# Four plane buffers for the table lookup, paid for with shared bias, Silu and output buffers

## Chip, cores and metric

One Trainium2 chip, all 8 of its cores. Each core runs the same program on its own part of the data. The metric is the device time of the slowest core, in microseconds (us). Shorter is better.

## What is computed

One transformer layer on x of shape (2, 4096, 2048), f32. After a layer norm, linear attention and a gated feed-forward are both applied to the normalised input and added to x. The feed-forward's weights come as indices (0 to 15) into a table of 16 values.

```python
xn = layernorm(x)                                # over the last axis, 2048
Q = relu(xn @ Wq.T + bq) * decay                 # 16 heads of 128
K = relu(xn @ Wk.T + bk) * decay
V = xn @ Wv.T + bv
KV = einsum('bhnd,bhne->bhde', K, V); Ksum = K.sum(axis=2)
Z = 1 / (einsum('bhnd,bhd->bhn', Q, Ksum) + 1e-6)
attn = (einsum('bhnd,bhde->bhne', Q, KV) * Z) @ Wo.T + bo
gate = xn @ lut[gate_idx].T                      # (5504, 2048) indices
up   = xn @ lut[up_idx].T
ffn  = (silu(gate) * up) @ lut[down_idx].T       # (2048, 5504) indices
out  = x + attn + ffn
```

## The kernel before

Each core owns 1024 rows of x, in 8 tiles of 128. It also computes K and V for all 4096 rows of its batch (32 tiles), so that no core needs anything of another. The work goes through stages with a barrier (`s_ph`) between them:

- Start: K and V weights are loaded and cast, and the biases `bk_bf`, `bv_bf` (L274, L275), each one row on one partition, are copied by ScalarE.
- A (K/V stage): for each of 32 tiles layer norm, transposes, K and V projections (L507, L519) and the sums over rows.
- B1: layer norm and transposes of the core's own 8 tiles, by VectorE and TensorE.
- B2: Q projection, 32 units of 16 matmuls (L699) and a bias matmul (L702), with `bq_bf` (L656); VectorE clears negative values (L717).
- B3: attention output for 8 tiles.
- B5a: output projection, 16 units of 32 matmuls (L911), with `bo_bf` (L853).
- B4 (gate/up stage): 43 chunks `ic` of 128 hidden units. For each and for both halves `h2` of the columns: 16 gate matmuls (L993), 16 up matmuls (L999), Silu by ScalarE (L1014), the multiplication by VectorE (L1026). TensorE's results have two buffers, so it is at most two chunks ahead of VectorE (L990).
- B5b (last stage): 4 quarters `q` of the output columns, for each 8 x 43 matmuls (L1104), then the addition of x (L1118) for 8 tiles `t` and the store (L1131).

**Weights from the table.** Beside all this the index blocks `k` = 0 to 128 (43 each for gate, up and down) are turned into bf16 weights of 128 x 2048, written to memory and read again in B4 and B5b. GpSimd (`g_front`) loads the indices of block k+1 (L126), casts those of block k (L134) and stores the weights of block k-1 (L171). There are two ways to look a block up:

- `g_vec`, VectorE alone (blocks 0 to 29 in stage A, 109 to 128 in B4): for each of 16 values a plane (the table value where the index equals v, else 0) and an addition, 15 pairs of L159 and L162.
- `g_vec_a` with `g_pe`, assisted by TensorE (79 blocks: 10 in B1, 22 in B2, 22 in B3, 25 in B5a): VectorE makes plane v (L205), TensorE adds it into PSUM with 4 matmuls against the identity (L222). `s_pl` counts planes made, `s_pm` planes consumed. After 16 planes VectorE copies PSUM to `wts` (L211). There are two plane buffers, so VectorE waits at L204 for the plane before the last. In all of these stages the loops on VectorE and TensorE carry the same blocks at the same places, between their other work, each engine's queue in program order.

In B4 the Silu results have one buffer for each half; ScalarE waits at L1013 for the multiplication of the same half of the chunk before. In B5b there are eight output buffers `xo8`. SyncE's queue holds for each quarter the 43 loads of weights (L1074), each waiting for the one before and for the matmuls three back, and then the 8 loads of x (L1084), each waiting for the one before it (L1083) and, from the second quarter on, for the store of the same tile of the quarter before (L1081). GpSimd's queue holds the stores, VectorE's the additions.

Of the kernel before, what the change touches and what calls it, by code (L numbers as in the profile page):

```python
# [16 lines left out]
D = 2048  # L17
# [16 lines left out]
def build():  # L34
# [38 lines left out]
    with es0:  # L73
# [14 lines left out]
        wts = [es0.enter_context(nc.sbuf_tensor(f"wt{i}", [128, D], BF16)) for i in range(2)]  # L88
        planes = [es0.enter_context(nc.sbuf_tensor(f"plane{i}", [128, D], BF16)) for i in range(2)]
        wt2 = es0.enter_context(nc.sbuf_tensor("wt2", [128, D], BF16))  # L90
# [106 lines left out]
        def g_vec_a(vector, k):  # L197
            a = AORD[k]
            gb = gbs[k % 2]
            vector.wait_ge(s_gc, VEC_IDX[k] + 1)  # L200
            for v in range(16):
                p = a * 16 + v
                if p >= 2:
                    vector.wait_ge(s_pm, p - 1)  # L204
                i = vector.tensor_scalar(planes[v % 2][:], gb[:], float(v),  # L205
                                         lutb[:, v : v + 1], ALU.is_equal, ALU.mult)
                inc(i, "s_pl", s_pl, 1)
            vector.wait_ge(s_pm, (a + 1) * 16)
            if k > 1:
                vector.wait_ge(s_go, 16 * (k - 1))  # L210
            i = vector.tensor_copy(wts[k % 2][:], PS_ACC[0][:])  # L211
            inc(i, "s_gv", s_gv, 1)

        def g_pe(tensor, k):
            a = AORD[k]
            ps_acc = PS_ACC[0]
            for v in range(16):
                tensor.wait_ge(s_pl, a * 16 + v + 1)
                if v == 0:
                    tensor.wait_ge(s_gv, k)  # L220
                for j4 in range(4):
                    i = tensor.matmul(ps_acc[:, j4 * 512 : (j4 + 1) * 512], eye_sb[:],  # L222
                                      planes[v % 2][:, j4 * 512 : (j4 + 1) * 512],
                                      start=(v == 0), stop=(v == 15), skip_group_check=True)
                inc(i, "s_pm", s_pm, 1)
# [47 lines left out]
        ps_tr = esA.enter_context(nc.psum_tensor("ps_tr", [128, 1024], BF16))  # L273
        bk_bf = esA.enter_context(nc.sbuf_tensor("bk_bf", [1, D], BF16))  # L274
        bv_bf = esA.enter_context(nc.sbuf_tensor("bv_bf", [1, D], BF16))  # L275

# [378 lines left out]
        xtb2 = [xtb2_0, xtb2_0]  # L655
        bq_bf = esB2.enter_context(nc.sbuf_tensor("bq_bf", [1, D], BF16))  # L656
        wbig = arena[:, 32768:65536].rearrange("p (a b) -> p a b", a=DC)
# [194 lines left out]
        xtb5 = [xtb5_0, xtb5_0]  # L852
        bo_bf = esB5a.enter_context(nc.sbuf_tensor("bo_bf", [1, D], BF16))  # L853
        wohalf = arena[:, 16384:32768].rearrange("p (a b) -> p a b", a=DC)
# [103 lines left out]
        w2b = [w2sb_, wt2]  # L958
        silu_sb = [esB4.enter_context(nc.sbuf_tensor(f"silu{i}", [128, 512], F32)) for i in range(2)]
        ps_g = [esB4.enter_context(nc.psum_tensor(f"ps_g{i}", [128, 1024], F32)) for i in range(2)]  # L960
# [4 lines left out]
        with nc.Block() as blk:  # L965
# [41 lines left out]
            def _(scalar):  # L1007
                bwait(scalar)
                for ic in range(IC):
                    for h2 in range(2):  # L1010
                        scalar.wait_ge(s_mm, MB4 + 4 * ic + 2 * h2 + 1)
                        if ic > 0:
                            scalar.wait_ge(s_ve, VB4 + 2 * (ic - 1) + h2 + 1)  # L1013
                        i = scalar.activation(silu_sb[h2][:], ps_g[ic % 2][:, h2 * 512 : (h2 + 1) * 512],  # L1014
                                              AF.Silu)
                        inc(i, "s_sc", s_sc, 1)
# [30 lines left out]
        w3qb = [arena[:, i * 512 : (i + 1) * 512] for i in range(NW3)]  # L1047
        xo8 = [esB5b.enter_context(nc.sbuf_tensor(f"xo8_{i}", [128, 512], F32)) for i in range(8)]
        ps8 = [esB5b.enter_context(nc.psum_tensor(f"ps8_{i}", [128, 512], F32)) for i in range(8)]
# [7 lines left out]
        with nc.Block() as blk:  # L1057
# [6 lines left out]
            def _(sync):  # L1064
                bwait(sync)
                for q in range(4):
# [10 lines left out]
                    for t in range(8):  # L1077
                        m = 8 * q + t
                        if q > 0:
                            n = (8 * (q - 1) + t - t % 2) // 2 + 1  # L1080
                            sync.wait_ge(s_oa[t % 2], 16 * n)  # L1081
                        if m >= 1:
                            sync.wait_ge(s_xo, XO0 + 16 * m)  # L1083
                        d = sync.dma_start(out=xo8[t][:],  # L1084
                                           in_=xo[t * 128 : (t + 1) * 128, q * 512 : (q + 1) * 512])
# [26 lines left out]
            def _(vector):  # L1112
                bwait(vector)
                for q in range(4):
                    vector.wait_ge(s_mm, MB5 + (IC + 1) * (q + 1))
                    for t in range(8):
                        vector.wait_ge(s_xo, XO0 + 16 * (8 * q + t + 1))  # L1117
                        i = vector.tensor_tensor(xo8[t][:], ps8[t][:], xo8[t][:], ALU.add)  # L1118
                        inc(i, "s_ve", s_ve, 1)
# [3 lines left out]
            def _(gpsimd):  # L1123
                bwait(gpsimd)
                for q in range(4):
                    for t in range(8):
                        gpsimd.wait_ge(s_ve, VB5 + 8 * q + t + 1)  # L1127
                        n = (8 * q + t - t % 2) // 2
                        if n > 0:
                            gpsimd.wait_ge(s_oa[t % 2], 16 * n)  # L1130
                        d = gpsimd.dma_start(out=y[t * 128 : (t + 1) * 128, q * 512 : (q + 1) * 512],  # L1131
                                             in_=xo8[t][:])
                        inc(d, f"s_out{t % 2}", s_oa[t % 2], 16)
# [69 lines left out]
```

## Time and profile before

| | us |
|---|---|
| timed runs, median (2 runs, 4982.36 to 4986.58) | 4984.47 |
| profiled execution | 5030.28 |
| its span, slowest core (core 3) | 5028.7 |
| spans of the 8 cores | 4965.5 to 5028.7 |
| start and K/V stage | 0 to about 1516 |
| B1, B2, B3, B5a | 1516 to about 3755 |
| B4 | 3755 to about 4508 |
| B5b | 4508 to 5028.7 |

PE is TensorE, PEld its weight loads, DVE VectorE, ACT ScalarE, POOL GpSimd, SP SyncE; a "q" behind a name is the engine's sequencer. PEclk is the granted TensorE clock, 1.00 being 2.4 GHz and 0.50 being 1.2 GHz. A row of instructions names line and operation, then what is written and read (out<-in, buffer numbers left out), then shapes and count. `[0.42 <-PE ps_acc L222]` behind a row of the timeline means that the engine sat idle for 0.42 us before it and that the instruction named released it. `x2` merges two instructions that follow each other; a merged row's length runs from the first start to the last end. The ends of matmuls are modelled and overlap the next one's start. A row of busy time by stretch gives the stretch (us from the start of the span) and its length, then the busy time (and instructions) of PE, PEld, DVE, ACT and POOL, then PEclk, the busy share of the DMA engines, and GB/s.

### The profile page before, as it was taken

Reading aid. Unit: us, or ns where it says so; the run is one execution under the profiler, and the core shown is the slowest. Engines: PE = TensorE matmul, PEld = TensorE weight load, DVE = VectorE, ACT = ScalarE, POOL = GpSimd, SP = SyncE. Lnnn points to the kernel's source line nnn. Section 1 sums busy time; section 2 is a strip of 40 time slices with the busy share of each in tenths; the row PEclk is TensorE's granted clock in tenths of the full one; section 3 lists DMA queues with packets and bytes.
Section 4 is the critical chain, followed back from the end, with each engine's and each line's share of the span. In section 5 each row is a group of like instructions: output and inputs, shape, how many; then the busy total and the mean of one; then the engine's idle time right before and its main releaser. Section 6 shows DMA issues by size and latency. Waiting matters only on the chain. (4 is left out here: it accounts for less than half of the span.)

```text
span 5028.7 us, 46175 instructions; the slowest of 8 cores (4965.5 to 5028.7 us)
## 1 busy us (share of the span) xinstructions
PE 3768.2 (75%) x16705; PEld 1494.3 (30%) x16705; DVE 3015.7 (60%) x3433; ACT 522.9 (10%) x715; POOL 411.6 (8%) x428
## 2 busy tenths in 40 slices
PE   0699998989885625888877772895889898866666
PEld 0233333333332211333322220332324333322222
DVE  0677786888855623666666662674767898970000
ACT  4222222222210011000000001001000000000000
POOL 0000000000000000111111110111110000000000
PEclk9888889999997767999888886998999999979988
DMA  7211111111101121000000002012112222212222
GB/s 245 82 40 45 44 45 38 45 45 44 51 21 54 51 95 71 32 32 32 32 32 32 32 32 82 33 44 76 37 50 80 84 86 87 83 52 78 78 76 76
DMA packets 91161, 297.99 MB, mean 59 GB/s; under 512 B 11639, under 2 KB 33655, under 8 KB 79673
## 3 DMA queue, kind: packets, MB, share of 16 engines
q1 hardware_dynamic: 59484, 185.19, 11.1%
q0 software_dynamic: 31456, 109.86, 6.3%
q8 instruction: 139, 2.28, 0.2%
q14 instruction: 82, 0.67, 0.0%
HBM read 218.98 MB, written 76.02 MB: 59 GB/s over the span
## 5 line engine op out<-in xcount | busy, mean ns | idle before, releaser
L222 PE MATMUL ps_acc<-plane,eye_sb 128*128 128x512 bf16 x5056 | 1299.1, 402 | 247.7 <-DVE plane L205 181.2
L205 DVE TENSOR_SCALAR plane<-gb,lutb 128x2048 bf16<-128x2048 bf16 x1264 | 1012.7, 807 | 553.2 <-PE ps_acc L222 502.3
L162 DVE TENSOR_TENSOR wt<-wt,plane 128x2048 bf16<-128x2048 bf16 x750 | 918.6, 1225 | 57.9 <-issue 2.6
L222 PEld LDWEIGHTS ps_acc<-plane,eye_sb 128*128 128x128 bf16 x5056 | 440.4, 101 | 1097.4 <-issue 814.0
L507 PE MATMUL ps_rot<-wk_bf,xnT_sb 128*128 128x512 bf16 x2048 | 557.0, 434 | 43.6 <-ACT xnT_sb L471 43.6
L159 DVE TENSOR_SCALAR plane<-gb,lutb 128x2048 bf16<-128x2048 bf16 x750 | 559.6, 746 | 0.0
L519 PE MATMUL ps_rot<-wv_bf,xnT_sb 128*128 128x512 bf16 x2048 | 489.1, 394 | 0.0
L1104 PE MATMUL ps<-arena 128*128 128x512 bf16 x1376 | 326.7, 382 | 79.5 <-DMA arena<-w2h 79.3
L1118 DVE TENSOR_TENSOR xo<-ps,xo 128x512 f32<-128x512 f32 x32 | 22.1, 692 | 496.5 <-PE ps L1104 426.2
L507 PEld LDWEIGHTS ps_rot<-wk_bf,xnT_sb 128*128 128x128 bf16 x2048 | 211.8, 108 | 351.7 <-issue 238.6
L519 PEld LDWEIGHTS ps_rot<-wv_bf,xnT_sb 128*128 128x128 bf16 x2048 | 194.9, 100 | 258.8 <-issue 102.1
L134 POOL CAST gb<-gi 128x2048 bf16<-128x2048 int8 x129 | 245.3, 1902 | 9.7 <-DMA gi<-g 7.2
L211 DVE CAST wt<-ps_acc 128x2048 bf16<-128x2048 f32 x79 | 181.0, 2291 | 106.4 <-PE ps_acc L222 106.4
L911 PE MATMUL ps_w<-arena 128*128 128x512 bf16 x512 | 117.2, 389 | 131.7 <-ACT arena L895 131.7
L699 PE MATMUL ps_q<-arena 128*128 128x512 bf16 x512 | 118.7, 386 | 120.8 <-ACT arena L684 120.8
L1104 PEld LDWEIGHTS ps<-arena 128*128 128x128 bf16 x1376 | 125.0, 98 | 281.8 <-issue 158.6
L993 PE MATMUL ps_g<-arena,KV_sb 128*128 128x512 bf16 x672 | 172.6, 416 | 46.6 <-DVE arena L1026 46.6
L993 PE MATMUL ps_g<-arena,w1sb 128*128 128x512 bf16 x704 | 173.4, 403 | 38.3 <-DVE arena L1026 28.6
L497 PE MATMUL ps_tr<-eye_sb,xn_bf 128*128 128x128 bf16 x512 | 42.8, 232 | 203.8 <-DVE xn_bf L259 134.4
L999 PE MATMUL ps_u<-arena,w2sb 128*128 128x512 bf16 x704 | 159.1, 379 | 0.0
L229 DVE TENSOR_REDUCE st<-xt 128x1 f32<-128x2048 f32 x32 | 73.1, 2286 | 141.7 <-DMA xt<-xb 135.8
L999 PE MATMUL ps_u<-arena,wt 128*128 128x512 bf16 x672 | 151.9, 379 | 0.0
(92 smaller groups left out, 1798.9 us busy)
## 6 DMA issues: line engine op xcount, KB each, us to landing
xt<-xb SPq DMA_DIRECT2D x32, 1024.0 KB, 4.9
gi<-g POOLq DMA_DIRECT2D x86, 256.0 KB, 3.8
w0h<-wt POOLq DMA_DIRECT2D x43, 512.0 KB, 3.0
w1h<-wt POOLq DMA_DIRECT2D x43, 512.0 KB, 3.0
w2h<-wt POOLq DMA_DIRECT2D x43, 512.0 KB, 3.0
arena<-w2h SPq DMA_DIRECT2D x172, 128.0 KB
xt<-wkT SPq DMA_DIRECT2D x16, 1024.0 KB, 5.6
xt<-wvT SPq DMA_DIRECT2D x16, 1024.0 KB, 5.5
```

The source lines that it names most:

```text
L134: i = eng.tensor_copy(gbs[k % 2][:], gi[k % 2][:])
L159: vector.tensor_scalar(planes[v % 2][:], gb[:], float(v), lutb[:, v : v + 1], ALU.is_equal, ALU.mult)
L162: vector.tensor_tensor(wt[:], wt[:], planes[v % 2][:], ALU.add)
L205: i = vector.tensor_scalar(planes[v % 2][:], gb[:], float(v), lutb[:, v : v + 1], ALU.is_equal, ALU.mult)
L211: i = vector.tensor_copy(wts[k % 2][:], PS_ACC[0][:])
L222: i = tensor.matmul(ps_acc[:, j4 * 512 : (j4 + 1) * 512], eye_sb[:], planes[v % 2][:, j4 * 512 : (j4 + 1) * 512], start=(v == 0), stop=(v ...
L507: tensor.matmul(ps_rot[j % 2][:], xnT_sb[:, dc * 128 : (dc + 1) * 128], wk_bf[:, dc, j * 512 : (j + 1) * 512], start=(dc == 0), stop=False)
L519: tensor.matmul(ps_rot[j % 2][:], xnT_sb[:, dc * 128 : (dc + 1) * 128], wv_bf[:, dc, j * 512 : (j + 1) * 512], start=(dc == 0), stop=False)
L699: tensor.matmul(pq[:], wbig[:, dc, qc * 128 : (qc + 1) * 128], xnT_own[:, dc, h2 * 512 : (h2 + 1) * 512], start=(dc == 0), stop=False)
L993: i = tensor.matmul(pg[:, h2 * 512 : (h2 + 1) * 512], w1b[ic % 2][:, dc * 128 : (dc + 1) * 128], xnT_own[:, dc, h2 * 512 : (h2 + 1) * 512] ...
L999: i = tensor.matmul(pu[:, h2 * 512 : (h2 + 1) * 512], w2b[ic % 2][:, dc * 128 : (dc + 1) * 128], xnT_own[:, dc, h2 * 512 : (h2 + 1) * 512] ...
L1104: i = tensor.matmul(ps8[t][:], hT_sl(ic, slice(t * 128, (t + 1) * 128)), w3qb[j % NW3], start=False, stop=(ic == IC - 1), skip_group_check ...
```

## The change

The planes get four buffers instead of two, and VectorE waits for the plane four back. The room comes from elsewhere: `bk_bf` and `bv_bf` become the first partition of planes 2 and 3, `bq_bf` and `bo_bf` that of `wt2`; both Silu halves share one buffer, and ScalarE waits for the multiplication just before; the output buffers of the last stage are four instead of eight, and the load of x for tile t waits for the store four tiles back. The instructions and their number are the same on every engine; only buffers and the values waited for differ.

```diff
--- before.py
+++ after.py
@@ -86,7 +86,7 @@
         gi = [es0.enter_context(nc.sbuf_tensor(f"gi{i}", [128, D], I8)) for i in range(2)]
         gbs = [es0.enter_context(nc.sbuf_tensor(f"gb{i}", [128, D], BF16)) for i in range(2)]
         wts = [es0.enter_context(nc.sbuf_tensor(f"wt{i}", [128, D], BF16)) for i in range(2)]
-        planes = [es0.enter_context(nc.sbuf_tensor(f"plane{i}", [128, D], BF16)) for i in range(2)]
+        planes = [es0.enter_context(nc.sbuf_tensor(f"plane{i}", [128, D], BF16)) for i in range(4)]
         wt2 = es0.enter_context(nc.sbuf_tensor("wt2", [128, D], BF16))
 
         KV_sb = es0.enter_context(nc.sbuf_tensor("KV_sb", [128, H * 128], BF16))
@@ -200,9 +200,9 @@
             vector.wait_ge(s_gc, VEC_IDX[k] + 1)
             for v in range(16):
                 p = a * 16 + v
-                if p >= 2:
-                    vector.wait_ge(s_pm, p - 1)
-                i = vector.tensor_scalar(planes[v % 2][:], gb[:], float(v),
+                if p >= 4:
+                    vector.wait_ge(s_pm, p - 3)
+                i = vector.tensor_scalar(planes[v % 4][:], gb[:], float(v),
                                          lutb[:, v : v + 1], ALU.is_equal, ALU.mult)
                 inc(i, "s_pl", s_pl, 1)
             vector.wait_ge(s_pm, (a + 1) * 16)
@@ -220,7 +220,7 @@
                     tensor.wait_ge(s_gv, k)
                 for j4 in range(4):
                     i = tensor.matmul(ps_acc[:, j4 * 512 : (j4 + 1) * 512], eye_sb[:],
-                                      planes[v % 2][:, j4 * 512 : (j4 + 1) * 512],
+                                      planes[v % 4][:, j4 * 512 : (j4 + 1) * 512],
                                       start=(v == 0), stop=(v == 15), skip_group_check=True)
                 inc(i, "s_pm", s_pm, 1)
 
@@ -271,8 +271,8 @@
         ps_ks = esA.enter_context(nc.psum_tensor("ps_ks", [128, H], F32))
         ps_rot = [esA.enter_context(nc.psum_tensor(f"ps_rot{b}", [128, 512], F32)) for b in range(2)]
         ps_tr = esA.enter_context(nc.psum_tensor("ps_tr", [128, 1024], BF16))
-        bk_bf = esA.enter_context(nc.sbuf_tensor("bk_bf", [1, D], BF16))
-        bv_bf = esA.enter_context(nc.sbuf_tensor("bv_bf", [1, D], BF16))
+        bk_bf = planes[2][0:1, 0:D]
+        bv_bf = planes[3][0:1, 0:D]
 
         with nc.Block() as blk:
             @blk.sync
@@ -653,7 +653,7 @@
         esB2 = contextlib.ExitStack()
         xtb2_0 = esB2.enter_context(nc.sbuf_tensor("xtb2_0", [128, D], F32))
         xtb2 = [xtb2_0, xtb2_0]
-        bq_bf = esB2.enter_context(nc.sbuf_tensor("bq_bf", [1, D], BF16))
+        bq_bf = wt2[0:1, 0:D]
         wbig = arena[:, 32768:65536].rearrange("p (a b) -> p a b", a=DC)
         ps_q = [esB2.enter_context(nc.psum_tensor(f"ps_q{i}", [128, 512], F32)) for i in range(4)]
         ps_acc2 = esB2.enter_context(nc.psum_tensor("ps_acc2", [128, 2048], F32))
@@ -850,7 +850,7 @@
         esB5a = contextlib.ExitStack()
         xtb5_0 = esB5a.enter_context(nc.sbuf_tensor("xtb5_0", [128, 1024], F32))
         xtb5 = [xtb5_0, xtb5_0]
-        bo_bf = esB5a.enter_context(nc.sbuf_tensor("bo_bf", [1, D], BF16))
+        bo_bf = wt2[0:1, 0:D]
         wohalf = arena[:, 16384:32768].rearrange("p (a b) -> p a b", a=DC)
         ps_w = [esB5a.enter_context(nc.psum_tensor(f"ps_w{i}", [128, 1024], F32)) for i in range(2)]
         ps_acc5 = esB5a.enter_context(nc.psum_tensor("ps_acc5", [128, 2048], F32))
@@ -956,7 +956,8 @@
         w2sb_ = esB4.enter_context(nc.sbuf_tensor("w2sb", [128, D], BF16))
         w1b = [w1sb_, KV_sb]
         w2b = [w2sb_, wt2]
-        silu_sb = [esB4.enter_context(nc.sbuf_tensor(f"silu{i}", [128, 512], F32)) for i in range(2)]
+        silu1 = esB4.enter_context(nc.sbuf_tensor("silu0", [128, 512], F32))
+        silu_sb = [silu1, silu1]
         ps_g = [esB4.enter_context(nc.psum_tensor(f"ps_g{i}", [128, 1024], F32)) for i in range(2)]
         ps_u = [esB4.enter_context(nc.psum_tensor(f"ps_u{i}", [128, 1024], F32)) for i in range(2)]
 
@@ -1009,8 +1010,8 @@
                 for ic in range(IC):
                     for h2 in range(2):
                         scalar.wait_ge(s_mm, MB4 + 4 * ic + 2 * h2 + 1)
-                        if ic > 0:
-                            scalar.wait_ge(s_ve, VB4 + 2 * (ic - 1) + h2 + 1)
+                        if ic > 0 or h2 > 0:
+                            scalar.wait_ge(s_ve, VB4 + 2 * ic + h2)
                         i = scalar.activation(silu_sb[h2][:], ps_g[ic % 2][:, h2 * 512 : (h2 + 1) * 512],
                                               AF.Silu)
                         inc(i, "s_sc", s_sc, 1)
@@ -1045,7 +1046,7 @@
         esB5b = contextlib.ExitStack()
         NW3 = 3
         w3qb = [arena[:, i * 512 : (i + 1) * 512] for i in range(NW3)]
-        xo8 = [esB5b.enter_context(nc.sbuf_tensor(f"xo8_{i}", [128, 512], F32)) for i in range(8)]
+        xo8 = [esB5b.enter_context(nc.sbuf_tensor(f"xo8_{i}", [128, 512], F32)) for i in range(4)]
         ps8 = [esB5b.enter_context(nc.psum_tensor(f"ps8_{i}", [128, 512], F32)) for i in range(8)]
 
         VB5, SB5, MB5 = C["s_ve"], C["s_sc"], C["s_mm"]
@@ -1076,12 +1077,12 @@
                         inc(d, "s_x0", s_xp[0], 16)
                     for t in range(8):
                         m = 8 * q + t
-                        if q > 0:
-                            n = (8 * (q - 1) + t - t % 2) // 2 + 1
+                        if m >= 4:
+                            n = (m - 4 - t % 2) // 2 + 1
                             sync.wait_ge(s_oa[t % 2], 16 * n)
                         if m >= 1:
                             sync.wait_ge(s_xo, XO0 + 16 * m)
-                        d = sync.dma_start(out=xo8[t][:],
+                        d = sync.dma_start(out=xo8[t % 4][:],
                                            in_=xo[t * 128 : (t + 1) * 128, q * 512 : (q + 1) * 512])
                         inc(d, "s_xo", s_xo, 16)
                 bdone(sync)
@@ -1115,7 +1116,7 @@
                     vector.wait_ge(s_mm, MB5 + (IC + 1) * (q + 1))
                     for t in range(8):
                         vector.wait_ge(s_xo, XO0 + 16 * (8 * q + t + 1))
-                        i = vector.tensor_tensor(xo8[t][:], ps8[t][:], xo8[t][:], ALU.add)
+                        i = vector.tensor_tensor(xo8[t % 4][:], ps8[t][:], xo8[t % 4][:], ALU.add)
                         inc(i, "s_ve", s_ve, 1)
                 bdone(vector)
 
@@ -1129,7 +1130,7 @@
                         if n > 0:
                             gpsimd.wait_ge(s_oa[t % 2], 16 * n)
                         d = gpsimd.dma_start(out=y[t * 128 : (t + 1) * 128, q * 512 : (q + 1) * 512],
-                                             in_=xo8[t][:])
+                                             in_=xo8[t % 4][:])
                         inc(d, f"s_out{t % 2}", s_oa[t % 2], 16)
                 gpsimd.wait_ge(s_oa[0], 16 * 16)
                 gpsimd.wait_ge(s_oa[1], 16 * 16)
```

## Rows read from the trace of the kernel before

**Rows 1.** The cores view: span and mean granted clock of cores 0 and 3.

```profile
core 0: 4976.6 us, clock 0.879
...
core 3: 5028.7 us, clock 0.882
```

**Rows 2.** Busy time by stretch: 180 to 620 us, core 0, then core 3.

```profile
180.00:620.00 440.00, 393.74 (x2024) 169.67 (x2024) 374.44 (x396) 104.48 (x165) 32.68 (x33) 0.93 0.14 47
...
180.00:620.00 440.00, 399.61 (x1821) 161.88 (x1820) 334.52 (x354) 94.29 (x149) 29.67 (x30) 0.81 0.11 40
```

**Rows 3.** Costliest groups: L222; count | busy us, mean ns | idle us <-releaser.

```profile
L222 PE MATMUL ps_acc<-plane,eye_sb 128*128 128x512 bf16 x5056 | 1299.1, 402 | 247.7 <-DVE plane L205 181.2
```

**Rows 4.** Timeline of full-clock bursts, PE and DVE: start, us, engine, what, idle before.

```profile
1995.94 1.41 DVE L205 TENSOR_SCALAR plane<-gb,lutb 128x2048 bf16<-128x2048 bf16 x2
1996.94 16.12 PE L222 MATMUL ps_acc<-plane,eye_sb 128*128 128x512 bf16 x64 [1.72 <-DVE plane L205]
...
2000.11 1.62 DVE L205 TENSOR_SCALAR plane<-gb,lutb 128x2048 bf16<-128x2048 bf16 x2 [0.42 <-PE ps_acc L222]
...
2002.14 1.61 DVE L205 TENSOR_SCALAR plane<-gb,lutb 128x2048 bf16<-128x2048 bf16 x2 [0.42 <-PE ps_acc L222]
...
3715.19 16.14 PE L222 MATMUL ps_acc<-plane,eye_sb 128*128 128x512 bf16 x64
```

**Rows 5.** Timeline of PE alone: K/V stage, a half-clock start, then projections of B2.

```profile
187.51 4.37 PE L507 MATMUL ps_rot<-wk_bf,xnT_sb 128*128 128x512 bf16 x16
...
2019.93 17.50 PE L222 MATMUL ps_acc<-plane,eye_sb 128*128 128x512 bf16 x64 [3.09 <-DVE plane L205]
2037.27 3.62 PE L699 MATMUL ps_q<-arena 128*128 128x512 bf16 x16
2040.81 0.38 PE L702 MATMUL ps_q<-ones_bf,bq_bf 1*128 1x512 bf16 x1
```

**Rows 6.** Stretch of the gate/up stage B4, core 3, same columns.

```profile
3755.00:4508.00 753.00, 632.06 (x2752) 276.33 (x2752) 643.11 (x707) 52.63 (x87) 59.29 (x60) 0.92 0.24 82
```

**Rows 7.** Waits of the whole run: who waited for whom, us, times, longest.

```profile
ACT silu L1014 <- DVE arena L1026: 390.7, 19, 22.3
...
PE ps_g L993 <- DVE arena L1026: 75.2, 18, 5.8
...
DVE arena L1026 <- PE ps_u L999: 72.8, 10, 14.8
```

**Rows 8.** Source view of L222: durations ns min/median/max; what its idle time waited for.

```profile
L222 PE MATMUL ps_acc<-plane,eye_sb x5056: 376/378/634, 1521.2 to 3751.9; 128*128 128x512 bf16 x195
...
  DVE plane L205: 181.2, 86
```

**Rows 9.** Timeline around a cast of GpSimd in a burst of B5a.

```profile
3262.89 1.90 POOL L134 CAST gb<-gi 128x2048 bf16<-128x2048 int8 x1
3262.97 3.04 DVE L205 TENSOR_SCALAR plane<-gb,lutb 128x2048 bf16<-128x2048 bf16 x2 [0.72 <-PE ps_acc L222]
...
3265.50 1.67 PE L222 MATMUL ps_acc<-plane,eye_sb 128*128 128x512 bf16 x7 [1.77 <-DVE plane L205]
```

**Rows 10.** Timeline of B4 behind a table block: DVE and ACT.

```profile
3836.29 1.28 DVE L1026 TENSOR_TENSOR arena<-silu,ps_u 128x512 bf16<-128x512 f32 x2 [0.26 <-issue]
...
3837.07 1.19 ACT L1014 ACTIVATE silu<-ps_g 128x512 f32<-128x512 f32 x2 [20.85 <-DVE arena L1026]
...
3837.84 1.28 DVE L1026 TENSOR_TENSOR arena<-silu,ps_u 128x512 bf16<-128x512 f32 x2 [0.27 <-ACT silu L1014]
...
3839.05 1.16 DVE L157 TENSOR_SCALAR wt<-gb,lutb 128x2048 bf16<-128x2048 bf16 x1
```

**Rows 11.** Timeline of B5b, first quarter: a store's issue, the fourth addition.

```profile
4616.09 0.54 POOL L1131 DMA_DIRECT2D y<-xo  x1 [110.80 <-DVE xo L1118]
...
4622.14 0.69 DVE L1118 TENSOR_TENSOR xo<-ps,xo 128x512 f32<-128x512 f32 x1 [2.07 <-DMA xo<-xo]
```

**Rows 12.** Source view of L1131: time from the issue of a store to landing.

```profile
DMA to landing us min/median/max: 2.3/2.9/4.4
```

## The prediction

> **What bounds the kernel now.** I read the views in this order: spans and clocks of the cores, the costliest groups, then the timeline inside each stage that the change touches.
>
> The cores differ, and this must be cleared away first. The profiled core is 3, some 50 us longer than core 0 [rows 1]. In 180 to 620 us, inside the K/V stage, core 3 was granted 0.81 of the TensorE clock and did 1821 matmuls where core 0 did 2024 [rows 2]. That is 203 fewer, at about 0.22 us each 44 us, nearly the whole difference. The stage is not touched by the change. The timed runs (median 4984.5) agree with the cores that escaped this. So I work out microseconds gained or lost on core 3 and subtract them both from its own time (span 5028.7 plus 1.6 around it, 5030.3) and from the median; the profile lies 45.8 above the median, and that offset has nothing to do with the change.
>
> The assisted table stages (B1, B2, B3, B5a) hold 79 bursts of 16 planes, 64 matmuls each: 5056 matmuls at L222, 1299 us of TensorE [rows 3]. VectorE makes a plane, TensorE adds it into PSUM with four identity matmuls, and the two are alone with each other. A burst at full clock shows who sets the pace [rows 4]: TensorE takes 16.12 us for 64 matmuls without a recorded pause, yet VectorE's pairs of planes start at 2000.11 and 2002.14, 2.03 us apart, so 1.017 us for each plane. TensorE alone could do better. Sixteen dense matmuls take 3.62 us and a lone one 0.38 [rows 5], so one starts each (3.62 - 0.38)/15 = 0.216 us and four need 0.864. VectorE could too: two planes with no wait end after 1.41 us, so they start 0.66 apart. Neither engine is full; the loop is. With two buffers, plane p+2 starts when the matmuls of p have ended: 2.03 us for making a plane, telling TensorE, four matmuls, and telling VectorE. The missing time is hidden in TensorE's modelled ends, and shows as VectorE's 0.42 us before each pair.
>
> In the gate/up stage (B4, 3755 to 4508 us) both engines are busy, VectorE 643 and TensorE 632 of 753 us, at granted clock 0.92 [rows 6]. Here the matmuls wait 18 times for VectorE, 75.2 us in total, and the Silu waits 19 times for it [rows 7]. Twenty table blocks of some 30 us each sit in VectorE's queue, and after all but the last a backlog of multiplications stands behind it. The last stage (B5b) comes in with its edit, below.
>
> **The change, part by part.**
>
> *Four planes.* Plane p now waits for the matmuls of p-4. The same loop of 2.03 us now serves four planes, 0.51 each, less than TensorE's 0.864, so TensorE becomes the bound. Saved at full clock: 1.017 - 0.864 = 0.153 us a plane. In a 16-plane burst the two-buffer loop runs seven times, so 7 x 2.03 becomes 14 x 0.864: 2.1 us. Where the granted clock is 0.5, a plane takes TensorE 1.7 us, above either loop, and nothing is saved. How many are those? A matmul lasts 378 ns (median) at full clock and up to 634 at half [rows 8], and the mean is 402 [rows 3]: (402 - 378)/(634 - 378) = 9.4%, or some 475 matmuls, 119 planes. So (79 x 14 - 119) x 0.153 = 151 us. Nothing lies beside it: each burst is waited for by VectorE's copy of PSUM, or by the projections behind it on TensorE, so a shorter burst moves all that follows. What stands between bursts (copy, first plane, normalisation, and the two waits for weights at the start of B2 and in B5a) stays as it is.
>
> *GpSimd's cast.* In some bursts the cast of the next indices (1.90 us) falls on the third plane, and two planes take 3.04 us instead of 1.62 [rows 4, 9]; TensorE sits idle 1.77 us. TensorE waited for a plane 86 times [rows 8], seven more than there are bursts. With four buffers two more planes are made before the cast begins. I take half of 7 x 1.77 = 12 us: 6 (0 to 12). Sum of the four stages: -157 us.
>
> *One Silu buffer.* Behind a table block the backlog is four multiplications. Now [rows 10] they start at 3836.29, then (two in 1.28 us) 0.6 later, 3837.84 and 0.6 later; the next block starts at 3839.05, 2.76 after the first. With one buffer each Silu waits for the multiplication before it and each multiplication for its Silu. That loop is seen: multiplication at 3836.29, Silu at 3837.07 (0.78 later), the next multiplication at 3837.84 (another 0.77). So 1.55 us a link; four multiplications start at 0, 1.55, 3.10, 4.65, and the next block at 4.65 + 0.6 = 5.25. Cost 5.25 - 2.76 = 2.5 us for each backlog, of which there are 19. TensorE already waits for VectorE at these places, so VectorE's queue is the path, except in the two places where three chunks lie between blocks and VectorE waits for TensorE (10 such waits: six ahead of the first block, two in each of these places) [rows 7]. 17 x 2.5 = +42 us. Queued behind a late multiplication are the next table block, GpSimd's store of it, and with that the last stage. Bounds: 0 if something hides it, 19 x 2.5 = 48 if nothing does.
>
> *Four output buffers.* The load of x tile t+4 now waits until tile t is stored. But SyncE already issues each load only when the one before has landed. In the first quarter the store of tile 0 was issued at 4616.09 [rows 11]; landing takes 2.9 us, at most 4.4 [rows 12], so 4619.0 to 4620.5. The load of tile 4 follows the landing of tile 3, which freed VectorE's addition at 4622.14. Slack is 1.6 to 3 us: cost 0. If that cover were gone, each of four quarters would pay a store's landing, some 4 x 3 = 12 us.
>
> *Bias rows in other buffers.* They hold memory that is idle in their stages, with the same copies and matmuls: 0.
>
> Sum: -157 + 42 + 0 = -115 us. Own time 5030.3 - 115 = 4915; against the median 4984.5 - 115 = **4869.5 us**, 2.3% faster.
>
> A point against denser bursts is the clock. Core 3 in K/V shows it: sixteen dense matmuls take 4.37 us instead of 3.62 [rows 5] at granted clock 0.81 [rows 2]. The Trainium skill (TensorE: Matmul & The Clock Gate, Part 1) says that dense matmuls on three cores of a die bring the whole die to 13/16 of the clock, and that all-zero data does not. By it the bursts, now dense, could run at 0.81 everywhere. The trace agrees in the figure, not in the reach: core 0 of the same die kept its clock in the same stretch.
>
> **The rivals.**
>
> *The bursts run at 0.81 (slower).* A plane would take 0.864 x 4.37/3.62 = 1.04 us, more than today's 1.017: 79 x 14 x 0.026 = +28, plus 42: 5055 us. It decides from a granted clock of 0.85 in the bursts (0.864/0.85 = 1.017). Against: B4's dense stretches keep 0.92 over all, pauses included, and a plane is mostly zeros (one index value in sixteen).
>
> *The loop does not open.* VectorE is the bound for another reason, or pays for running close behind GpSimd; a plane stays at 1.017 us. Then 4984.5 + 42 = 5027. Against: the 0.66 us between unforced starts.
>
> *The clock falls more often.* A burst with a half-clock start took 17.50 instead of 16.12 [rows 4, 5]: such a stretch costs 1.4 us. 24 of the 79 bursts ran at 16.1 us, the first at 1996.94 and the last at 3715.19 [rows 4]. If shorter bursts between the same pauses lose those, +24 x 1.4 = 34: 4904.
>
> *The clock falls less often*, since TensorE is denser. All 475 slow matmuls made fast would give 475 x 0.216 = 103; half of it 51: 4818.
>
> *The Silu loop is hidden* by TensorE's wait: 4869.5 - 42 = 4827.
>
> **How the numbers follow.** A measurement here tells about 2% from no change; 2% is 4884.8. Chances: my forecast 0.60, 0.81 clock 0.04, loop stays 0.06, clock falls more 0.13, less 0.08, Silu hidden 0.09. The forecast's own range is 4850 to 4890 (Silu's and the cast's bounds, ten planes in a hundred more or fewer at half clock), so 0.06 of its 0.60 lies within 2%. The 0.81 case, 5055, is 1.4% slower; over 2% it is only if the last two stages drop to that clock as well, half of it. Faster 0.54 + 0.08 + 0.09 = 0.71; within 2% 0.06 + 0.06 + 0.13 + 0.02 = 0.27; slower by more 0.02. The range 4820 to 4905 leaves out the two upper cases, 0.10, and about 0.09 at its ends.
>
> **What would show it.** In a full-clock burst plane starts must be 0.86 us apart and a burst 14.0 us long instead of 16.1; VectorE's 0.42 us before a pair turns into a wait before each plane of about 0.1. The 3.04 us pair must vanish or cost TensorE under 1 us. In B4 there must be 1.55 us between all four multiplications of a backlog, TensorE's 75 us of waiting must grow by about 40, and the stage must be 42 us longer. B5b and the K/V stage must not move beyond what their clock explains. I am wrong if the bursts keep 16 us, if their granted clock is under 0.85, or if B4 grows by less than 20 us.

## The result and the profile after

| | before | after |
|---|---|---|
| ratio after / before, 95% interval | | 0.9718 (0.9679 to 0.9757) |
| profiled execution | 5030.3 us | 4841.5 us |
| spans of the 8 cores in it | 4965.5 to 5028.7 | 4803.3 to 4840.0 |

The kernel is 2.8% faster; on the 4984.5 us of before that is 141 us, and 4844 us. The ratio leaves out the executions of either kernel that ran longer while the cores of one die were granted a lower clock, and so it can't be had from the plain median of the changed kernel's eleven executions, 4959.6.

Stage by stage, mean over the 8 cores of the two profiled executions. "Table stages" runs from the first plane of B1 to the last copy out of PSUM in B5a, B4 from its first gate matmul to the first matmul of the last stage.

| stage | before | after | change | forecast |
|---|---|---|---|---|
| table stages | 2229.5 us | 2044.1 us | -185.4 | -157 |
| B4 | 748.8 | 784.9 | +36.1 | +42 |
| last stage | 521.5 | 513.8 | -7.7 | 0 |

The start with the K/V stage is not in the table: on the six cores of before other than 2 and 3 [rows 2] it ends at 1446 us on average, after the change at 1448.

Core 0 of both executions shows this in rows. First before, then after: the source view of L222 (durations in ns, the first and last start; what its own idle time waited for, us and times; who waited for it), of the gate matmuls (L993, now L994) and of the first matmuls of the last stage (L1096, now L1097).

```profile
L222 PE MATMUL ps_acc<-plane,eye_sb x5056: 376/378/634, 1463.1 to 3684.5; 128*128 128x512 bf16 x195
...
  DVE plane L205: 180.7, 84
...
  DVE wt L211: 106.4, 79
...
L993 PE MATMUL ps_g<-arena,w1sb x704: 376/379/634, 3693.4 to 4397.9; 128*128 128x512 bf16 x176
...
L1096 PE MATMUL ps<-arena,eye_sb x32: 413/631/634, 4442.1 to 4840.8; 128*128 128x512 bf16 x32
```

```profile
L222 PE MATMUL ps_acc<-plane,eye_sb x5056: 376/379/634, 1466.8 to 3511.7; 128*128 128x512 bf16 x195
...
  DVE plane L205: 166.2, 64
...
  DVE wt L211: 218.8, 79
...
L994 PE MATMUL ps_g<-arena,w1sb x704: 376/379/634, 3520.9 to 4255.7; 128*128 128x512 bf16 x176
...
L1097 PE MATMUL ps<-arena,eye_sb x32: 380/631/634, 4305.6 to 4698.2; 128*128 128x512 bf16 x32
```

The plane matmuls stretch over 2221 us before (1463.1 to 3684.5) and 2045 after. From the first gate matmul to the last stage it is 748.7 and 784.7. VectorE's copy out of PSUM waits 218.8 us for the matmuls now, where it waited 106.4 on this core before (79 copies each): VectorE is done with its planes early and TensorE is the one that is waited for.

A burst at full clock after the change, VectorE and TensorE of core 2 (start, length, engine, what, count, idle before):

```profile
1919.16 12.39 DVE L205 TENSOR_SCALAR plane<-gb,lutb 128x2048 bf16<-128x2048 bf16 x16
1934.31 2.29 DVE L211 CAST wt<-ps_acc 128x2048 bf16<-128x2048 f32 x1 [2.77 <-PE ps_acc L222]
...
1920.16 13.97 PE L222 MATMUL ps_acc<-plane,eye_sb 128*128 128x512 bf16 x62 [1.72 <-DVE plane L205]
```

13.97 us instead of 16.12 [rows 4]. VectorE's sixteen planes are one unbroken row of 12.39 us; its pauses of 0.42 us before each pair are gone, and it waits 2.77 us at the end where it waited 1.34. By the start times in the trace of core 0 the first seven planes of such a burst start 0.66 us apart, as unforced ones did, and from the eighth on one starts every 0.86 us: by then VectorE has used up its buffers and goes at TensorE's pace, with the wait of about 0.1 us before each plane that the forecast named.

The gain lies inside the bursts. Summed over the 79 bursts, first to last matmul start, they take 1350 us before and 1161 after, 190 less, while the stretches between them are 4 us longer (mean of cores 0, 1, 3, 5, 6 and 7, whose records of these matmuls are complete).

### The profile page after: what moved, and what is told of

Same layout as the page of the kernel before. It is cut to its first block and busy times, and to the rows that moved or that the text cites. A ratio compares the mean times of both kernels' runs of the same rounds, so it can differ in the third digit from the quotient of the medians.

```text
span 4840.0 us, 45872 instructions; the slowest of 8 cores (4803.3 to 4840.0 us)
## 1 busy us (share of the span) xinstructions
PE 3571.5 (74%) x16399; PEld 1551.9 (32%) x16705; DVE 3004.0 (62%) x3433; ACT 523.1 (11%) x715; POOL 415.3 (9%) x428
## 5 line engine op out<-in xcount | busy, mean ns | idle before, releaser
L222 PE MATMUL ps_acc<-plane,eye_sb 128*128 128x512 bf16 x4947 | 1181.6, 400 | 176.7 <-DVE plane L205 171.6
L222 PEld LDWEIGHTS ps_acc<-plane,eye_sb 128*128 128x128 bf16 x5056 | 509.5, 102 | 840.1 <-issue 313.3
L507 PE MATMUL ps_rot<-wk_bf,xnT_sb 128*128 128x512 bf16 x1985 | 517.0, 419 | 60.2 <-ACT xnT_sb L471 55.3
L519 PE MATMUL ps_rot<-wv_bf,xnT_sb 128*128 128x512 bf16 x2015 | 457.1, 379 | 5.0 <-issue 4.9
L211 DVE CAST wt<-ps_acc 128x2048 bf16<-128x2048 f32 x79 | 181.0, 2292 | 218.8 <-PE ps_acc L222 218.8
L994 PE MATMUL ps_g<-arena,KV_sb 128*128 128x512 bf16 x659 | 171.7, 417 | 63.9 <-DVE arena L1027 62.9
L994 PE MATMUL ps_g<-arena,w1sb 128*128 128x512 bf16 x689 | 175.0, 408 | 50.7 <-DVE arena L1027 39.9
```

The lines of the kernel that those rows point to most:

```text
L507: tensor.matmul(ps_rot[j % 2][:], xnT_sb[:, dc * 128 : (dc + 1) * 128], wk_bf[:, dc, j * 512 : (j + 1) * 512], start=(dc == 0), stop=False)
L519: tensor.matmul(ps_rot[j % 2][:], xnT_sb[:, dc * 128 : (dc + 1) * 128], wv_bf[:, dc, j * 512 : (j + 1) * 512], start=(dc == 0), stop=False)
L994: i = tensor.matmul(pg[:, h2 * 512 : (h2 + 1) * 512], w1b[ic % 2][:, dc * 128 : (dc + 1) * 128], xnT_own[:, dc, h2 * 512 : (h2 + 1) * 512] ...
```

## The experiments

Three things of the forecast can be tried one at a time: that the gain is the round of a plane through its buffer, that the price in B4 is the single Silu buffer's alone, and that the output buffers are free. The rivals: each further buffer shortens the round a little; B4's growth comes from other buffers moved; the last stage gains or loses by its four output buffers.

### One Silu buffer alone

```diff
 before
-        silu_sb = [... for i in range(2)]
+        silu1 = ...; silu_sb = [silu1, silu1]
-                        if ic > 0:
-                            scalar.wait_ge(s_ve, VB4 + 2 * (ic - 1) + h2 + 1)
+                        if ic > 0 or h2 > 0:
+                            scalar.wait_ge(s_ve, VB4 + 2 * ic + h2)
```

> The kernel before with one change alone: both Silu halves share one buffer, as in the changed kernel. Theory (the Silu loop is the price): B4, counted from its first gate matmul to the first matmul of the last stage, grows by 17 x (2.5 - 0.4) = 36 us over the 748 to 750 us of before, the 0.4 being the cast that no longer falls on the first plane of the next block; the whole kernel is 36 us (0.7%) longer, all other stages as before. Rival (the growth of B4 comes from elsewhere, such as the moved buffers): B4 within 5 us of before, the kernel the same.

Measured: ratio 1.0064 (1.0041 to 1.0087), B4 785.4 us on average of the cores. The source views of its core 0:

```profile
L994 PE MATMUL ps_g<-arena,w1sb x689: 377/380/635, 3709.5 to 4444.0; 128*128 128x512 bf16 x173
...
L1097 PE MATMUL ps<-arena,eye_sb x31: 547/632/635, 4494.0 to 4888.8; 128*128 128x512 bf16 x31
```

3709.5 to 4494.0 are 784.5 us, those of the changed kernel to 0.2. The growth of B4 is the Silu buffer's and nobody else's. The chain is seen in the changed kernel, core 0, timeline behind a table block:

```profile
3595.25 0.69 DVE L1027 TENSOR_TENSOR arena<-silu,ps_u 128x512 bf16<-128x512 f32 x1 [0.26 <-issue]
...
3596.03 0.60 ACT L1015 ACTIVATE silu<-ps_g 128x512 f32<-128x512 f32 x1 [27.77 <-DVE arena L1027]
...
3596.08 5.14 PE L994 MATMUL ps_g<-arena,KV_sb 128*128 128x512 bf16 x16 [4.40 <-DVE arena L1027]
...
3596.71 1.90 POOL L134 CAST gb<-gi 128x2048 bf16<-128x2048 int8 x1
3596.80 0.69 DVE L1027 TENSOR_TENSOR arena<-silu,ps_u 128x512 bf16<-128x512 f32 x1 [0.86 <-ACT silu L1015]
...
3597.58 0.60 ACT L1015 ACTIVATE silu<-ps_g 128x512 f32<-128x512 f32 x1 [0.95 <-DVE arena L1027]
...
3598.35 0.69 DVE L1027 TENSOR_TENSOR arena<-silu,ps_u 128x512 bf16<-128x512 f32 x1 [0.86 <-ACT silu L1015]
...
3599.13 0.60 ACT L1015 ACTIVATE silu<-ps_g 128x512 f32<-128x512 f32 x1 [0.95 <-DVE arena L1027]
...
3599.90 0.69 DVE L1027 TENSOR_TENSOR arena<-silu,ps_u 128x512 bf16<-128x512 f32 x1 [0.86 <-ACT silu L1015]
3600.51 0.75 DVE L157 TENSOR_SCALAR wt<-gb,lutb 128x2048 bf16<-128x2048 bf16 x1
```

The four multiplications start 1.55 us apart and the next block (L157) 5.26 after the first, against 2.76 before [rows 10]. The forecast had 5.25. It had missed one thing, and the same rows have it: before, GpSimd's cast (here 3596.71 to 3598.61) lay across the next block's first operation, which took 1.16 us [rows 10], and so in 15 of the 20 blocks on core 0. Now the cast is over by then and that operation takes 0.75. So a backlog costs 2.5 - 0.4 = 2.1 us, 17 of them 36 us, as measured.

### Four planes with two Silu buffers

```diff
 after
-        w1sb_ = ...; w2sb_ = ...
-        w1b = [w1sb_, KV_sb]; w2b = [w2sb_, wt2]
+        w1b = [planes[2], KV_sb]; w2b = [planes[3], wt2]
-        silu1 = ...                     (and its wait)
+        silu_sb = [... for i in range(2)]     (and the wait of before)
```

> The changed kernel with two Silu buffers again; the room is had by letting B4's staging tiles for gate and up weights use planes 2 and 3, which are idle there. Theory: B4 is back to 748 to 750 us, the table stages keep their shorter time (from the first to the last instruction of the assisted blocks about 2045 us, before 2230), the kernel is 36 us shorter than the changed one: about 4805 us, ratio to before 0.964. Rival (the staging tiles in planes, or four planes, cost something in B4): B4 stays near 785 us, ratio 0.971.

Measured: ratio 0.9623 (0.9595 to 0.9651). The source views of its core 0:

```profile
L222 PE MATMUL ps_acc<-plane,eye_sb x4947: 375/380/635, 1468.5 to 3512.7; 128*128 128x512 bf16 x198
...
L991 PE MATMUL ps_g<-arena,plane x689: 376/380/635, 3522.0 to 4223.3; 128*128 128x512 bf16 x173
...
L1094 PE MATMUL ps<-arena,eye_sb x31: 381/631/632, 4270.3 to 4660.1; 128*128 128x512 bf16 x31
```

The plane matmuls stretch over 2044 us as in the changed kernel, and B4 is back to 748.3. The whole gain stands without the price. The room for the fourth plane was there all along: `g_vec` uses planes 0 and 1 alone, so the other two are free in B4.

### Four output buffers alone

```diff
 before
-        xo8 = [... for i in range(8)]            xo8[t]
+        xo8 = [... for i in range(4)]            xo8[t % 4]
-                        if q > 0:
-                            n = (8 * (q - 1) + t - t % 2) // 2 + 1
+                        if m >= 4:
+                            n = (m - 4 - t % 2) // 2 + 1
```

> The kernel before with four output buffers in the last stage alone. Theory (the loads of x are paced by each other's landing, the new wait is met earlier): the tails of the four quarters stay at 21 to 27 us, the kernel is the same within 5 us. Rival one (the store four tiles back holds the load up): about 3 us more a quarter, 12 in all. Rival two (fewer loads and stores overlap, so that each lands sooner): tails 2 to 4 us shorter, some 10 us in all, as the tails of the changed kernel look.

Measured: ratio 0.9986 (0.9928 to 1.0045), last stage 520.3 us on average of the cores, before 521.5. The edit costs nothing, as forecast. Whether it gains a few us stays open. A quarter's tail runs from the end of its last matmul to the end of its last addition. The four tails sum to 93.9 us before and 89.7 in the kernel with one Silu buffer, both with eight output buffers. With four output buffers they sum to 85.9 after the change, 87.2 with four planes and two Silu buffers, 89.8 in this kernel, and 89.8 with three planes and two Silu buffers (mean of the 8 cores, one execution each). The two groups touch, and the 8 us of the table above are within that.

### Three planes

```diff
 after
-        planes = [... for i in range(4)]         planes[v % 4]
+        planes = [... for i in range(3)]         planes[p % 3]   (p = 16 a + v)
-                if p >= 4:
-                    vector.wait_ge(s_pm, p - 3)
+                if p >= 3:
+                    vector.wait_ge(s_pm, p - 2)
-        bv_bf = planes[3][0:1, 0:D]
+        bv_bf = KV_sb[0:1, 0:D]
```

> The changed kernel with three planes instead of four. Theory (a loop of 2.03 us through the buffers): three buffers give 2.03 / 3 = 0.68 us a plane, still less than TensorE's 0.864, so plane starts stay at 0.86 us and a full-clock burst at 14.0 us; only where GpSimd's cast falls into a burst is there less cover, at most 22 x 0.7 = 15 us. The kernel is 0 to 15 us longer than the changed one. Rival (each further buffer shortens the loop in proportion because several waits overlap): a plane between 0.86 and 1.02, say 0.94, so 79 x 14 x 0.08 = 88 us longer than the changed one.

There is no ratio for this kernel. Its profiled execution is read on core 7, at mean granted clock 0.891. Source view of L222:

```profile
L222 PE MATMUL ps_acc<-plane,eye_sb x5056: 376/379/634, 1475.4 to 3519.3; 128*128 128x512 bf16 x195
```

1475.4 to 3519.3 are 2044 us, as with four planes. The same with two Silu buffers, for which three planes leave the room, was then measured for itself:

```diff
 the kernel with three planes
-        silu1 = ...                     (and its wait)
+        silu_sb = [... for i in range(2)]     (and the wait of before)
```

> Three planes and two Silu buffers; B4's staging tiles stay where the changed kernel has them (three planes leave room for the second Silu buffer). Theory: three buffers give all of the gain and the second Silu buffer takes away the price, so this equals the run with four planes and two Silu buffers: ratio to before 0.962 to 0.964, table stages about 2045 us, B4 748 us. Rival (the fourth plane is worth something where the cast falls into a burst): 10 to 15 us longer, ratio 0.965 or more.

> The kernel of the run before once more (three planes, two Silu buffers), since that execution was profiled at granted clocks down to 0.32 and says nothing on stages. Theory: equal to four planes and two Silu buffers: ratio 0.962 to 0.964, table stages about 2045 us, B4 748 us. Rival (the fourth plane is worth something under the casts): ratio 0.965 or more.

The first of these runs has no ratio either: one of its executions took 10839 us at mean granted clocks down to 0.32, and of the other three the shortest took 4794.5. Measured in the second: ratio 0.9627 (0.9604 to 0.965), four planes had 0.9623. Timeline of its core 0, a full-clock burst, then the source view of L222, then that of the gate matmuls and of the last stage's first:

```profile
1999.24 13.25 DVE L205 TENSOR_SCALAR plane<-gb,lutb 128x2048 bf16<-128x2048 bf16 x16
...
2000.24 13.97 PE L222 MATMUL ps_acc<-plane,eye_sb 128*128 128x512 bf16 x62 [1.72 <-DVE plane L205]
...
L222 PE MATMUL ps_acc<-plane,eye_sb x4947: 376/379/634, 1468.0 to 3512.4; 128*128 128x512 bf16 x198
...
L993 PE MATMUL ps_g<-arena,w1sb x689: 376/379/634, 3521.4 to 4225.3; 128*128 128x512 bf16 x173
...
L1096 PE MATMUL ps<-arena,eye_sb x31: 380/631/631, 4269.9 to 4665.4; 128*128 128x512 bf16 x31
```

A burst of 13.97 us, 2044 us of plane matmuls, B4 748.5 us. Within the intervals, some 0.3%, a third buffer gives everything and a fourth nothing: 2.03/3 = 0.68 is already under TensorE's 0.864. That is what a round through buffers predicts, and what "each buffer helps a little" does not. VectorE's row of sixteen planes is longer with three (13.25 us against 12.39), since it uses up its buffers sooner, but TensorE's is not.

### What is left in B4

With planes and Silu out of the way, B4 is still VectorE's. Four Silu buffers instead of two (one for each half of two chunks):

> Four planes (staging tiles of B4 in planes 2 and 3) and four Silu buffers, one for each half of two chunks. Theory (the backlog behind a table block is a chain through the Silu buffers): with no Silu waiting, the four multiplications start 0.6 us apart and the next block 2.4 us after the first instead of 2.76 with two buffers; 17 x 0.36 = 6 us off B4, so about 742 us where two buffers have 748. Rival: the cast that then falls wholly on the next block's first operation takes that back, B4 at 748. Either way the whole kernel is within 0.2% of the one with two buffers.

Measured: 0.9626 (0.9529 to 0.9724), B4 745 to 749 us on cores 4 to 7, at mean granted clock 0.89. The forecast of 742 was missed: it is worth nothing, or 1 us. The kernels that follow build on it. The first moves four table blocks from B4 to B5a (`GB5a` to 113, `GB4` from 113), the second makes two more in the K/V stage as well (`GA` to 32):

> The kernel with four planes and four Silu buffers, and four table blocks more (109 to 112) moved from B4, where VectorE alone makes them, to the assisted ones of B5a. Theory: B4 is set by VectorE's 20 blocks; with 16 blocks on 43 chunks TensorE (43 x 13.8 = 593 us) is the bound in most gaps, B4 falls from about 745 to 640 us; B5a grows by 4 x 18.5 = 74 us (burst 14.6, copy 2.3, first plane and signals). Sum -31 us, ratio to before about 0.956. Rival: the extra blocks in B5a cost more, or B4 keeps VectorE as its bound (over 690 us): no gain or a loss.

> The same with 32 instead of 30 blocks in the K/V stage, one for each tile, and 8 instead of 10 in B1. Theory: a tile of the K/V stage takes TensorE 40 us and VectorE about 36 with a block, so the two come free; B1 is 2 x 19 = 38 us shorter, ratio to before about 0.948. Rival: VectorE in the K/V stage is late for the next tile's layer norm, each of the two tiles pays up to 10 us.

Measured: 0.9723 (0.9603 to 0.9842) and 0.97 (0.9649 to 0.9751). Both forecasts were missed. These intervals overlap with that of the kernel without the moves, but the spans show that both are slower: 4841 to 4871 us and 4824 to 4855 on the 8 cores of the profiled executions, against 4785 to 4795 on cores 4 to 7 without the moves. B5a did grow, by 76 us where 74 were expected, but B4 fell by 20 us only, to 727 on average, where 640 was expected. Waits of core 0 with four blocks moved (us in total, times, longest):

```profile
DVE arena L1024 <- PE ps_u L997: 179.8, 26, 13.6
...
PE ps_g L991 <- DVE arena L1024: 62.2, 14, 5.1
```

VectorE now idles 180 us for want of TensorE, and TensorE still waits 14 times, nearly once for each of the 16 blocks. A whole block is 30 us and TensorE may be ahead by two chunks, 27.6, so nearly every block stops it, however few there are. In the K/V stage the two blocks were not free either: it ends at 1476 us on average of the cores instead of 1448, and B1, with two blocks less, is 34 us shorter (38 were expected), so that little is left. The likely reason is that there the engines depend on each other within a tile. Waits of the K/V stage on core 0, first the changed kernel, then this one:

```profile
PE ps_tr L497 <- ACT xnT_sb L471: 71.3, 32, 10.4
```

```profile
PE ps_tr L497 <- ACT xnT_sb L471: 97.3, 32, 36.1
```

So the blocks are cut, and then moved:

```diff
 the kernel with four Silu buffers
-                    for k in g_slice(GB4, ic, IC):
-                        g_vec(vector, k)
+                    for k, half in g_slice([(k, h) for k in GB4 for h in range(2)], ic, IC):
+                        g_vec_half(vector, k, half)     # v = 0..7, then 8..15
```

> The kernel with four planes and four Silu buffers; in B4 each of VectorE's 20 table blocks is cut in two halves of about 15 us and the halves are spread over the 43 chunks. Theory (B4 is held up because a block of 30 us is longer than the two chunks, 27.6 us, that TensorE may run ahead): no half is longer than that lead, TensorE's 75 to 100 us of waiting for VectorE goes, and B4 is VectorE's sum, 40 x 15.2 + 43 x 1.2 = 660 us, plus its ends: 665 to 680 instead of 745. Ratio to before about 0.948. Rival (B4 is VectorE's sum already and the order does not matter): B4 stays over 730 us.

> The same with blocks 109 and 110 moved to B5a. Theory: with halves in B4 VectorE's sum falls by 2 x 30.5 = 61 us towards TensorE's 43 x 13.8 = 593, so B4 is 615 to 635 us; B5a grows by 2 x 19 = 38. Sum -20 us against the unmoved one, ratio to before about 0.944. Rival: as with four blocks moved whole, B5a pays and B4 gives back less than 38 us.

Measured: cut alone 0.9602 (0.9569 to 0.9635), B4 735 us instead of 747. The forecast of 665 to 680 was wrong, and its rival came true: B4 is VectorE's sum already. TensorE still waits for it 26 times, 69.6 us in all on core 0. Timeline of core 0, from the end of one block to the start of the next:

```profile
3823.80 1.29 DVE L1041 TENSOR_TENSOR arena<-silu,ps_u 128x512 bf16<-128x512 f32 x2 [0.25 <-issue]
...
3825.01 2.71 DVE L173 TENSOR_SCALAR wt<-gb,lutb 128x2048 bf16<-128x2048 bf16 x1
3825.26 1.90 POOL L134 CAST gb<-gi 128x2048 bf16<-128x2048 int8 x1
```

VectorE has no gap here, and in all of B4 it waits only 32 us for TensorE, so its sum is the bound. That sum was mis-sized: the first operation of most blocks takes 2.71 us instead of 0.75, because GpSimd's cast of 1.90 us runs across it, and each chunk's pair of multiplications costs 1.45 with its wait: 20 x (30.5 + 2.0) + 43 x 1.45 = 712 of the 735 us. So each block moved should be worth 32 us. Measured with two moved: B4 667 us on cores 0 to 3, 68 less, 34 a block, B5a some 40 longer, ratio 0.9534 (0.9493 to 0.9575). The forecast, still with the smaller sum, had 615 to 635 us and 0.944. And with four moved:

> Four planes, four Silu buffers, B4's table blocks in halves, and four of them (109 to 112) moved to B5a; the earlier run with two moved had B4 at 667 us and a ratio of 0.953. Theory (B4 is VectorE's sum of about 34 us a block, down to TensorE's 43 x 13.8 = 593): two more moved take 2 x 34 = 68 off VectorE, so TensorE becomes the bound, B4 about 605 us; B5a grows by another 38. Sum -24, ratio 0.949. Rival (TensorE still waits for halves that fall between its chunks): B4 stays above 630, ratio 0.953 or more.

Measured: B4 623 us on cores 0 to 3 (forecast 605), ratio 0.9522 (0.9486 to 0.9559), where the forecast had 0.949. Source view of the gate matmuls, core 0, and VectorE's waits:

```profile
L1008 PE MATMUL ps_g<-arena,KV_sb x672: 379/379/379, 3613.5 to 4176.2; 128*128 128x512 bf16 x168
...
DVE arena L1041 <- PE ps_u L1014: 62.4, 19, 14.9
```

TensorE is the bound now: the list of waits holds none of its gate matmuls for VectorE, VectorE waits 62 us for it, and of the gate matmuls of every second chunk (672 of them) none ran at half clock: shortest, median and longest are 379 ns. B5a takes back nearly all of it, as B4's 44 us less cost 37 there, so the two kernels can't be told apart by their ratios. Either is faster than both kernels of this study: 0.953 and 0.952 against 1 and 0.972.

## Why the forecast came out as it did

Forecast: 4869.5 us, 2.3% faster, range 4820 to 4905. Measured: 2.8%, 4844 on the same footing. The likeliest case was the right one, and both of its mechanisms were shown one at a time.

**Right, term by term.** Burst 16.12 to 13.97 (forecast 14.0), plane to plane 0.86; the round of 2.03 us, shown by three planes being as good as four. Silu chain 5.26 us against 5.25. Output buffers 0, within some us. The bias rows were not tried alone: that they cost 0 is argued from the stretches between bursts, which hold the bias matmuls and grew by 4 us in all. TensorE's waiting in B4 grew by 28 us, less than the 40 of the forecast, as the waits of core 0 show, before and after:

```profile
PE ps_g L993 <- DVE arena L1026: 78.2, 18, 6.2
```

```profile
PE ps_g L994 <- DVE arena L1027: 105.8, 18, 6.7
```

B4 grew by 36, and most of the other 8 us lie behind its last matmul: the wait of the last stage's first matmul at the barrier grew from 40.4 to 46.0 us on core 0.

**The cast, mis-sized on a wrong count.** The forecast took 6 us, half of seven waits of 1.77, the seven being 86 waits less 79 bursts. That reading is wrong. Only 63 of these waits are for the first plane of a burst, in both kernels (the first plane of the others is ready in time). The rest stand inside bursts: 23 on core 3 before, most of them under 1 us. On the mean of the six cores named above they sum to 16.5 us before and 3.0 after, so the term is 13.5 us, just above the upper bound of 12. The 84 waits of core 0 became 64 in this way: 21 inside bursts became one.

What is left is seen where a whole burst runs at full clock with a cast in it (core 0 after the change):

```profile
1578.96 13.58 DVE L205 TENSOR_SCALAR plane<-gb,lutb 128x2048 bf16<-128x2048 bf16 x16
...
1581.14 1.90 POOL L134 CAST gb<-gi 128x2048 bf16<-128x2048 int8 x1
...
1583.75 11.38 PE L222 MATMUL ps_acc<-plane,eye_sb 128*128 128x512 bf16 x52 [1.04 <-DVE plane L205]
```

Three planes are ready when the cast begins, the fourth is late, and TensorE waits 1.04 us, where it waited 1.77 before [rows 9]; the forecast had named under 1. There are one to five such waits on a core. With three planes the wait is the same, 1.04. In most bursts with a cast in them TensorE's first matmuls ran at half clock, so that it was later than the late plane. So in this burst of core 2, then the granted clock (PEclk, third number from the end) of its first 3 and its last 10 us:

```profile
3065.10 13.88 DVE L205 TENSOR_SCALAR plane<-gb,lutb 128x2048 bf16<-128x2048 bf16 x16
...
3067.28 1.90 POOL L134 CAST gb<-gi 128x2048 bf16<-128x2048 int8 x1
3067.33 14.25 PE L222 MATMUL ps_acc<-plane,eye_sb 128*128 128x512 bf16 x60 [0.22 <-DVE plane L205]
...
3066.00:3069.00 3.00, 2.69 (x6) 1.04 (x8) 3.00 (x3) 0.00 (x0) 3.00 (x3) 0.50 0.56 193
3072.00:3082.00 10.00, 9.95 (x47) 4.49 (x47) 6.58 (x10) 0.00 (x0) 0.00 (x0) 1.00 0.00 0
```

**The clock, left out of the sum.** Steps from one plane matmul to the next of 0.43 us, the pace of 1.2 GHz, are 446 a core before and 349 after, mean of the same six cores; 97 x 0.216 = 21 us. The forecast had this as a rival ("the clock falls less often", 51 us), and two fifths of it came true beside the main case. With it the table stages add up on these cores: 151 + 13.5 + 21 = 185.5 of the 186 us that the plane matmuls' stretch is shorter; that it fits so closely is luck, as the 151 are worked out and not counted. Why the clock fell less often was not tried. That TensorE's bursts are denser is the likely reason, and stays an argument. The price of the other clock rival rested on a wrong count too: 19 bursts of core 3 ran at 16.1 us, not 24. By the cast and the clock the measured 4844 lies outside the forecast's own 4850 to 4890, though inside the range.

**B4, 42 against 36.** The difference is the cast that no longer meets the next block, 17 x 0.4 = 7 us. It is the same collision that the forecast had looked at in the table stages and not in B4.

**The rivals that fell.** The bursts at 0.81 of the clock: the window row above has 1.00 and the burst 13.97 us, the pace of 0.216 a matmul. The rule of the Trainium skill (TensorE: Matmul & The Clock Gate, Part 1), by which dense matmuls on three cores of a die bring the whole die to 13/16, did not hold for these bursts; whether that is because a plane is mostly zeros was not tried. The closed loop: plane to plane 0.86. The Silu chain hidden: the kernel with it alone is 0.64% slower.

## What to carry to other kernels

Count the round through a buffer (produce, signal, consume, signal) and divide by the number of buffers: as soon as that is under the busier engine's time a piece, one more buffer buys nothing. Here three did what four did, and what had been given up for the fourth cost a fifth of the gain in the table stages. Before shrinking one buffer for another, look which buffers are idle in the stage that pays. And an engine that shares its queue between long blocks and short services stops its client whenever one block is longer than the client's lead, as long as its own sum leaves it time. Here fewer blocks alone took B4 from 747 to 727 us, shorter ones alone to 735, and both together to 623.

## What was not expected of the hardware

- GpSimd's cast (1.90 us, int8 to bf16) and VectorE's table operation (128x2048 bf16) exclude each other nearly in full: an operation of 0.75 us took 2.71 where the cast began 0.25 us after it. VectorE's multiplication of 128x512 from f32 is not touched: it took 0.69 us under a cast as elsewhere (the one at 3596.80 above). The collision showed in the bursts and in the first operation of B4's blocks, and moved the result in both.
- In the profiled execution of before, cores 2 and 3 ran 440 us of the K/V stage (180 to 620) at granted clock 0.81, while core 0 of the same die had 0.93 with the same work [rows 2]. In that of the changed kernel all 8 cores had 0.92 or 0.93 there.
